# A decoder layer on one core: the experts' gate and up products turned round, and two tiles of the attention's output prepared before the attention ends

## The reference

```python
x = x + attn(_layernorm(x), W_qkv, W_out)           # 16 heads of 64, rotary, causal mask, softmax
x = x + xattn(_layernorm(x), ctx, ctx, Wq, ..., Wo) # a memory M per head, scanned over 64 context rows; out = M q, Wo, bo
x = x + ffn(_layernorm(x), router_w, router_b, we_gate, we_up, we_down)

# ffn: 8 experts, top 2 of them for each token
ff_gate = ragged_dot(sorted_tokens, we_gate, group_sizes)
ff_up = ragged_dot(sorted_tokens, we_up, group_sizes)
ff_out = ragged_dot(silu(ff_gate) * ff_up, we_down, group_sizes)
out = zeros.at[sorted_token_idx].add(ff_out * sorted_weights[:, None])
```

## Time and profile before

| | |
|---|---|
| median of 3 runs | 2870.94 us (2869.32 to 2877.44) |
| the profiled execution | 2874.91 us |
| its span | 2873.2 us |
| mean granted clock of TensorE | 0.973 |
| PE, DVE, ACT, POOL busy | 93%, 70%, 56%, 51% of the span |

### The profile page before, as it was taken

The page is one execution under the profiler, slowest core; times in us unless marked ns, Lnnn a source line. Parts: engine busy times, 40 slices in busy tenths (PEclk is TensorE's granted clock), DMA queues, the critical chain, the costliest instruction groups (busy, mean ns, idle before and its releaser), DMA issues. The chain is left out here.

```text
span 2873.2 us, 48962 instructions
## 1 busy us (share of the span) xinstructions
PE 2665.0 (93%) x15375; PEld 2267.7 (79%) x15375; DVE 2000.5 (70%) x4223; ACT 1620.8 (56%) x3157; POOL 1468.0 (51%) x1676
## 2 busy tenths in 40 slices
PE   7999989999899999899998599999959999999997
PEld 5888878888788888788887487877748888888886
DVE  6777766777667777677777688978846556666655
ACT  3666666666656666566666333333336666666665
POOL 3676646676647675556565333434323444343434
PEclk9999999999999999999999799999979999999999
DMA  6654544444544444444444654544334443444433
GB/s 175 106 122 106 123 103 98 118 113 104 132 96 99 115 107 114 103 109 100 94 91 114 170 135 134 158 134 147 96 126 96 102 87 74 102 99 100 100 52 51
DMA packets 192360, 316.56 MB, mean 110 GB/s; under 512 B 60496, under 2 KB 106224, under 8 KB 189104
## 3 DMA queue, kind: packets, MB, share of 16 engines
q1 hardware_dynamic: 148656, 216.86, 31.6%
q0 software_dynamic: 43520, 97.46, 13.9%
HBM read 241.08 MB, written 75.17 MB: 110 GB/s over the span
## 5 line engine op out<-in xcount | busy, mean ns | idle before, releaser
L1095 ACT ACTIVATE a_pt<-a_PT 128x512 fp32r<-128x512 f32 (+3 forms) x768 | 350.4, 491 | 449.9 <-PE a_PT L962 443.3
L1226 DVE TENSOR_TENSOR a_pt<-a_PT,a_pt 128x512 fp32r<-128x512 f32 (+3 forms) x768 | 401.5, 550 | 155.2 <-ACT a_pt L1095 150.7
L1216 DVE CUSTOM_DVE_ANT_0 a_S<-a_S,a_mask 128x1024 f32<-128x1024 f32 (+7 forms) x512 | 387.5, 757 | 72.5 <-PE a_S L951 71.1
L1084 ACT ACTIVATE a_pb<-a_S,a_nmax 128x1024 f32<-128x1024 f32 (+7 forms) x512 | 381.0, 744 | 36.5 <-DVE a_nmax L1216 36.5
L962 PE MATMUL a_PT<-early_ident,a_pb 128*128 128x128 f32 x2304 | 345.0, 276 | 51.2 <-DVE a_pt L1226 50.9
L962 PEld LDWEIGHTS a_PT<-early_ident,a_pb 128*128 128x128 f32 x2304 | 275.9, 142 | 112.4 <-issue 58.5
L979 PE MATMUL a_O<-a_pt,a_v 128*128 128x256 f32 (+1 forms) x2560 | 346.5, 283 | 17.8 <-DVE a_xt L1201 16.8
L979 PEld LDWEIGHTS a_O<-a_pt,a_v 128*128 128x128 f32 x2560 | 330.4, 193 | 31.2 <-DVE a_xt L1201 24.0
L2193 DVE TENSOR_TENSOR e_w<-early_stage,e_w 128x1024 fp32r<-128x1024 f32 x238 | 280.6, 1220 | 65.0 <-ACT e_w L2142 64.9
L950 PE MATMUL a_S<-a_kh,a_qs 128*128 128x512 f32 (+3 forms) x768 | 286.7, 373 | 10.6 <-DMA a_kl<-a_rot 8.8
L951 PE MATMUL a_S<-a_kl,a_qs 128*128 128x512 f32 (+3 forms) x768 | 259.0, 349 | 0.0
(11 more groups left out here) (305 smaller groups left out, 6890.2 us busy)
## 6 DMA issues: line engine op xcount, KB each, us to landing
a_qs<-a_rot SPq DMA_DIRECT2D x256, 128.0 KB, 2.4
a_kh<-a_rot SPq DMA_DIRECT2D x256, 128.0 KB, 2.4
a_kl<-a_rot SPq DMA_DIRECT2D x256, 128.0 KB, 2.4
e_rows<-scr_hs SPq DMA_DIRECT2D x40, 516.0 KB
scr_attT<-a_ot SPq DMA_DIRECT2D x256, 64.0 KB, 2.2
m_att<-scr_attT SPq DMA_DIRECT2D x32, 512.0 KB
m_rb<-scr_rinv SPq DMA_DIRECT2D x64, 256.0 KB
early_stage<-in_wqk POOLq DMA_DIRECT2D x31, 512.0 KB
```

Source lines behind the costliest of these rows:

```text
L1084: act.activation(pb[u % 2][:, 0:cols], S[u % 2][:, 0:cols], ACT.Exp, bias=nmax[:, u % GU:u % GU + 1], scale=-1.0, accum_out=rsum[:, b % 2, ...
L1095: act.activation(pt[u % 2][:, 0, 4 * s:4 * s + m, (qt % 2) * P:(qt % 2 + 1) * P], PT[(k + s) % 2][:, 0:m * P].rearrange("p (k q) -> p k q" ...
L1216: dve.tensor_tensor_reduce(out=sc, in0=sc, in1=mask[:, T - cols:T], scale=-1.0, scalar=-MASKED, op0=ALU.add, op1=ALU.min, accum_out=nmax[: ...
L1226: dve.tensor_tensor(pt[u % 2][:, 1, 4 * s:4 * s + m, q], PT[(k + s) % 2][:, 0:m * P].rearrange("p (k q) -> p k q", k=m), pt[u % 2][:, 0, 4 ...
```

## The change

In the attention and the memory stage:

- The tensor `rot` becomes `early["rot"]` and outlives the attention; the memory stage's `ap` (the split attention output of two tiles) lies in it.
- The last batch's sums are turned in unit U + 2 instead of U + 4.
- In units U - 13 and U - 11 SP loads the attention output and the sums of tiles 0 and 1 (`load_front`) into buffers that are free by then; POOL scales them in units U - 8 and U - 6, ACT makes the high parts in U + 1 and U + 2, DVE the low parts in U + 2 and U + 3.
- The four pieces of W_out are split in the last units too: high parts by ACT in U - 7, U - 5, U - 3, U - 1, low parts by POOL in U - 5, U - 3, U - 1, U + 1, into `xT`. POOL's loop runs to U + 2 for it.
- The memory stage no longer does any of this, PE waits for the constants only before the memory products, and in the second step PE transposes the first tile's n2 behind the first half of the second tile's product with W_out, not ahead of it. SP loads x of tiles 0 and 1 and then tile 2's attention output first.

In the experts:

- Gate and up have the weights as the stationary operand and 256 rows moving, so their results have features along the partitions and need no transposes for down. A half h is now 256 features of all 256 rows, not 128 rows.
- The engines' orders within a block change, and POOL's `fetch(0)` comes before `add_rows(0)`. DVE's wait for `added` with the small work comes before `mult(j, 0)`.

The diff, cut to its core:

```diff
         def sums_turn(u):
-            if u >= GU * G and u % (GU * G) == 4:
+            if u == U + 2:
+                return B - 1
+            if GU * G <= u < U and u % (GU * G) == 4:
                 return u // (GU * G) - 1
...
+        FRONT_IN = (U - 13, U - 11)
+        FRONT_SCALE = (U - 8, U - 6)
+        TAIL_HIGH = (U - 7, U - 5, U - 3, U - 1)
+        TAIL_LOW = (U - 5, U - 3, U - 1, U + 1)
...
+            def load_front(j):
...
+                sp.dma_start(front_rows(j), dram["attT"][j:j + 1, :, :].rearrange("o p (f t) -> p (o f) t", t=P)
+                             ).then_inc(s_first[j], 16)
+                for a in range(2):
+                    sp.dma_start(front_sums(j)[a * 64:(a + 1) * 64, :],
+                                 dram["rinv"][j, a:a + 1, :].rearrange("a n -> (a n)").partition_broadcast(64)
+                                 ).then_inc(s_first[j], 16)
             for u in range(U + 6):
                 if values_turn(u - 1) is not None:
                     store(values_turn(u - 1))
+                if u in FRONT_IN:
+                    load_front(FRONT_IN.index(u))
...
+            def front_scale(j):
+                gp.wait_ge(s_first[j], 48)
+                rows = front_rows(j)
+                gp.tensor_tensor(rows, rows, front_sums(j).rearrange("p (f t) -> p f t", t=P),
+                                 ALU.mult).then_inc(s_fscale, 1)
+            def tail_low(k):
+                gp.wait_ge(s_wmhi, k + 1)
+                gp.tensor_tensor(xT[:, 1, k, :], tail(k), xT[:, 0, k, :].bitcast(F32),
+                                 ALU.subtract).then_inc(s_wmlo, 1)
-            for u in range(U):
+            for u in range(U + 2):
...
+                if u in FRONT_SCALE:
+                    front_scale(FRONT_SCALE.index(u))
+                if u in TAIL_LOW:
+                    tail_low(TAIL_LOW.index(u))
...
             # attention, ACT
+                if u in TAIL_HIGH:
+                    tail_high(TAIL_HIGH.index(u))
+                if u in (U + 1, U + 2):
+                    front_high(u - U - 1)
             # attention, DVE
+                if u in (U + 2, U + 3):
+                    front_low(u - U - 2)
...
             # memory stage, PE
-            pe.wait_ge(s["pool"], 18)
+                second = isinstance(r, int) and r * QT + i == 1
+                if here(r, i - 1) and not second:
                     turn("n", 1, n2[:, (i - 1) % 2, :], "n2")
...
                     att_out(0, 4)
+                if second:
+                    turn("n", 1, n2[:, (i - 1) % 2, :], "n2")
...
             # experts, POOL
-                wait_alone(gp, s["y"], 2 * j + 1 + CR, s["any"])
-                add_rows(0)
                 wait_alone(gp, s["ix"], j + 2, s["any"])
                 wait_alone(gp, s["wlo0"], 2 * j + 4, s["any"])
                 fetch(0)
+                wait_alone(gp, s["y"], 2 * j + 1 + CR, s["any"])
+                add_rows(0)
...
             # experts, PE
+            def product(j, k, out, h, sem):
+                if h == 0:
+                    pe.wait_ge(s[f"wlo{k}"], 2 * j + 2)
+                if k == 0:
+                    pe.wait_ge(s["tlo"], 2 * j + RT + CR)
+                    pe.wait_ge(s["mul"], 2 * j + h - 1 + CR)
+                for f in range(2 * h, 2 * h + 2):
+                    for e in range(ET):
+                        c = e * D + f * P
+                        mm = parts(out[h][:, f % 2 * BLK:(f % 2 + 1) * BLK], lambda a: w[:, k, a, c:c + P],
+                                   lambda a: hT[:, a, e, :], e)
                 mm.then_inc(s[sem], 1)
+            def down(j, t, h):
+                pe.wait_ge(s["alo"], 2 * j + h + 1 + CR)
...
                 product(j, 0, pG, 0, "G")
+                product(j, 0, pG, 1, "G")
                 product(j, 1, pU, 0, "U")
-                product(j, 0, pG, 1, "G")
-                turn_act(j, 0)
                 product(j, 1, pU, 1, "U")
+                down(j, 0, 0)
                 turn_rows(j + 1, 0)
-                down(j, 0, 0, 2)
-                turn_act(j, 1)
-                down(j, 0, 2, ET).then_inc(s["Y"], 1)
+                down(j, 1, 0)
                 turn_rows(j + 1, 1)
-                down(j, 1, 0, ET).then_inc(s["Y"], 1)
+                down(j, 0, 1)
+                down(j, 1, 1)
             # experts, ACT
                 silu(j, 0)
                 silu(j, 1)
+                weight_high(j + 1, 0, "G")
                 act_high(j, 0)
-                weight_high(j + 1, 0, "G")
+                act_high(j, 1)
                 turn_high(j + 1, 0)
                 act.wait_ge(s["arg"], j + 1)
                 act.activation(gate[:, :], arg[:, :], ACT.Tanh).then_inc(s["gate"], 1)
-                act_high(j, 1)
+                turn_high(j + 1, 1)
                 weight_high(j + 1, 1, "U")
                 act.wait_ge(s["wt"], j + 1)
                 row_out(j, 0)
-                turn_high(j + 1, 1)
                 row_out(j, 1)
                 weight_high(j + 1, 2, "Y")
             # experts, DVE
                 for h in range(2):
                     weight_low(j, 2, h)
-                mult(j, 0)
-                act_low(j, 0)
-                mult(j, 1)
                 dve.wait_ge(s["added"], j + 1)
...
                 keep_side(j + 1)
+                mult(j, 0)
+                act_low(j, 0)
                 weight_low(j + 1, 0, 0)
+                mult(j, 1)
+                act_low(j, 1)
                 turn_low(j + 1, 0)
-                act_low(j, 1)
+                weight_low(j + 1, 0, 1)
                 dve.wait_ge(s["gate"], j + 1)
                 dve.tensor_scalar(wt[:, :], gate[:, :], 0.5, 0.5, ALU.mult, ALU.add).then_inc(s["wt"], 1)
-                weight_low(j + 1, 0, 1)
+                turn_low(j + 1, 1)
                 for h in range(2):
                     weight_low(j + 1, 1, h)
-                turn_low(j + 1, 1)
```

More of the change, by code:

```diff
@@ L506, in attention_phase @@
         s_wm = rm.sem("wm")
+        s_wmhi = rm.sem("wmhi")
+        s_wmlo = rm.sem("wmlo")
+        s_first = [rm.sem(f"first{i}") for i in range(2)]
+        s_fscale = rm.sem("fscale")
+        s_fhi = rm.sem("fhi")
+        s_flo = rm.sem("flo")
         s_scan = rm.sem("scan")
@@ L731, in _ @@
                                  ).then_inc(s_k2, 16)
+            def load_front(j):
+                i = NG * GH // 2 - 1
+                if j == 0:
+                    for k in range(2):
+                        sp.wait_ge(s_xst[k], 16 * QT * (B - 1))
+                    for k in range(4):
+                        sp.wait_ge(s_ost[k], 16 * NPAIR // B // 4)
+                    sp.wait_ge(s_rst, 16)
+                    sp.wait_ge(s_zfull, zi[("q", i, 3)] + 1)
+                else:
+                    sp.wait_ge(s_radd, 4 * (i + 1))
+                sp.dma_start(front_rows(j), dram["attT"][j:j + 1, :, :].rearrange("o p (f t) -> p (o f) t", t=P)
[4 more added lines that the diff above has]
+                                 ).then_inc(s_first[j], 16)
             for u in range(U + 6):
@@ L1105, in key_root, with tail_high, front_high @@
                 act.activation(kst[1], kst[0], ACT.Sqrt).then_inc(s_ksd, 1)
+            def tail_high(k):
+                act.wait_ge(s_wm, 96)
+                act.activation(xT[:, 0, k, :], tail(k), ACT.Copy).then_inc(s_wmhi, 1)
+            def front_high(j):
+                act.wait_ge(s_fscale, j + 1)
+                for sl in range(2):
+                    act.wait_ge(s_stack[sl], 192 * (NG * GH // 2))
+                act.activation(front[:, j, 0, :, :], front_rows(j), ACT.Copy).then_inc(s_fhi, 1)
             key_root(0)
@@ L1697, in _ @@
             act.sem_inc(s["hT"], CR)
[L1698 to L1701, removed]
+            act.sem_inc(s["ahi"], CR + 2)
             def att_high(r, j):
                 t = r * QT + j
-                act.wait_ge(s["an"], t + 1)
+                act.wait_ge(s["an"], t - 1)
                 act.wait_ge(s["x2"], t - 1 + CR)
@@ L1736, in step @@
                 memory_high(1)
-                if here(r, i + 1):
+                if here(r, i + 1) and after(r, i + 1, 2):
                     att_high(r, i + 1)
@@ L1769, in _ @@
         def _(dve):
-            for k in ("x2", "x3", "alo", "nlo", "qn", "rt", "pos", "mwl"):
+            for k in ("x2", "x3", "nlo", "qn", "rt", "pos", "mwl"):
                 dve.sem_inc(s[k], CR)
+            dve.sem_inc(s["alo"], CR + 2)
             dve.sem_inc(s["st30"], 16)
@@ L1790, in centre @@
                 dve.wait_ge(s["wc"], n + 3)
[L1792 to L1795, removed]
             def att_low(r, j):
@@ L2073, in turn_rows @@
                 pe.wait_ge(s["rows"], 16 * (j + 1))
-                pe.wait_ge(s["tlo"], 2 * j + t + CR)
+                pe.wait_ge(s["tlo"], 2 * j + t - 1 + CR)
                 for e in range(ET):
-                    mm = pe.transpose(pT[1][:, e * P:(e + 1) * P], rows[:, t, e * P:(e + 1) * P], ident[:, :])
```

(10 more changed lines are left out.)

108 lines of the change are left out of this document (57 added, 51 removed).

## The result

The kernel after took 2916.36 us (median of 4 runs, 2910.89 to 2920.65), the kernel before beside it 2871.64: ratio 1.0151, 95% interval 1.0139 to 1.0163. It is 45 us slower where 15 less were forecast, and outside the range. The profiled execution took 2920.65, its span is 2918.9, against 2873.2 before.

What follows compares the result with a forecast made beforehand. PE was taken to bound the experts, with the new block at 18.4 us set by the chain through `added`. Experts -5, weight changes +3, boundary -13 made -15 against 2874.9: 2860, median 2857; whole range 2834 to 2892.

Steps and rivals of the forecast that it cites:

- PE's sum: Experts: two transpose groups go (-0.86), narrower gate and up products add 0.32; PE's block 17.98 instead of 18.52 us.
- The loop through `added`: Experts: down product, row output, stores, landing, DVE's wait, next down product take 18.4 us a block; -0.12 x 39 = -5.
- The price of a change of weights: Experts: at seven changes of expert the second store lands late, about 0.4 us each remaining; +3 in all.
- the second store taken as free: Experts: POOL's second store, tried at 10.48, was summed without blocking by DVE, in a block of 18.4 us.
- rival A: Experts: DVE's lowering blocks the second store, adding 0.8; block 19.2, +27 over 39 blocks, median 2888; chance 0.28.
- the landing: Experts: second store lands 4.9 us after its start, at 15.38; `added` follows by 0.2.
- The last leg: Experts: from `dest` to the next down product: 0.62, three operations together 2.04, and 0.2 for hand-overs.
- the boundary: Attention's end to memory stage: opening 4.7 us later, 18 won after it; net -13, bounds -9 and -18.
- The bounds, +1 and +7: Memory stage's opening, +4.7 us forecast: +1 if the main chain ends last, +7 at 2.83 per POOL operation.
- +22 to +25: Memory stage: PE turns the second tile's normalised rows this many us after the opening, instead of 41.9; -18.
- C: Experts: the chain doesn't bind and PE sets the block, 17.98; -21 there, -34 in all, median 2837; chance 0.25.
- D: Boundary gives nothing: POOL's tail at +7, loads late, PE cold; with block 18.4, median 2870; chance 0.07 including what else.

Runs made afterwards that it cites:

- e4: Kernel after with DVE waiting for both gate products before the second half of the down weights' lowering: 2893.7 us, ratio 1.0079 to the kernel before.
- e2: Kernel after with the expert stage of the kernel before, so the new boundary alone: 2874.4 us, ratio 1.0010 to the kernel before.
- e9: Kernel after, order kept, with the memory's store issued by SP instead of POOL: 2911.1 us, ratio 1.0128 to the kernel before.
- e5: Kernel after with POOL's last two scan rows and memory store ahead of the first tile's scaling: 2899.7 us, ratio 1.0096 to the kernel before.
- e8: e6 with POOL's scaling of the third tile ahead of its wait for the six constants: 2826.7 us, ratio 0.9845 to the kernel before.
- e3: Kernel after with DVE's wait for `added` and its small operations moved behind mult(j,1): 2846.6 us, ratio 0.9912 to the kernel before.
- e6: Kernel after with the changes of e3 and e5 together: 2834.0 us, ratio 0.9870 to the kernel before.

## Why the prediction was wrong

**What held.** PE's sum: 17.83 a block once nothing waits, 17.98 forecast. The 48 gate products in 5.68 (2453.31 to the first up product at 2458.99) are 0.118 apart; 96 of them are 11.36, so the narrow form costs 0.16 more and not 0.32, which is the whole difference. By the rule of the Trainium skill (TensorE: Matmul & The Clock Gate, Back-to-back issue gap) the estimate was 0.12 more and a block of 17.78: nearer in the difference, but the rule's spacing itself, 0.109, is further from the measured 0.118 than my 0.120 of the earlier trace rows. The loop through `added` was the right one, the order on ACT came as computed (weight_high at +4.46, row_out(0) at +6.26; 4.36 and 6.16 forecast), the first store was blocked (2.45), and the second was tried at 10.56 (10.48). The price of a change of weights was less than forecast: from first down product to first down product the blocks exceed their median by 2.3 in all, and by 1.1 before the change, so 1.2 more where the sum has 3.

**The step that failed first: the second store taken as free.** "Mine is 0.09 after" was written of rival A and is what happened: the store was tried 0.04 to 0.24 after DVE's second lowering had begun, in 37 of the 38 blocks seen whole (it took 2.43 to 2.64 there; 1.58 in the one other). The deciding margin was under the errors of the sum, and every error in it was systematic, so the 39 blocks fell on one side together; the forecast should have been A. The Trainium skill (SBUF — State Buffer, SBUF: two separate sides) says that whichever starts first, an operation of DVE with two inputs in SBUF or one of GpSimd that reads SBUF, holds the port that they share for its whole length, and the other waits. For DVE's side the trace agrees: the store takes 2.62 beside the lowering and 1.58 without (e4). For the store the other side isn't seen: where it began 0.18 ahead, DVE's pair of lowerings kept its 2.36 and the store took 1.73. A's price, 0.8, was 0.60.

**The second: the landing.** I added 4.9, the median over all transfers of `out`, and 0.2. Unblocked, from the store's start to `dest` is 5.31, where 5.1 was forecast, and blocked 5.91. In the trace of before the profile tells the landing of second stores alone, 4.27 after the first store's start; in e4 the second store begins 2.76 after the first and, unblocked, lands at 5.24 (median). Whether the nearer first store delays it, no run shows. The last leg, from `dest` to the down product, took 3.01; the prediction's terms for it add up to 2.86, and their sum of 18.44 was rounded to 18.4. The sum: 18.44 + 0.08 (start) + 0.60 (blocked) + 0.21 (landing and hand-over) + 0.15 (last leg) = 19.48, against 19.51 measured. The three small terms all went the same way; with the rounding they are 0.48, and in a loop that is walked 39 times that is 19 us.

**Third: the boundary, -13 forecast, about +3 measured** (e2). The opening was forecast at 1599.9 and came at 1613.49:
- The memory's store went at 1603.69, not 1596.4 (the terms as written, 1570 + 25.8, give 1595.8: the 0.6 of the store's second half is in the 1599.9 twice). The broadcast load that was said to "queue behind that stack" at no cost let POOL start at 1573.20 and not 1567. It landed 14.2 (median) after its issue, behind 3 MB of memory weights that POOL had asked for 8 us earlier, with the DMA engines full up to then (share 1.01 from 1553 to 1573). And one scan step's row of additions took 5.07 instead of 2.29. These are 6.2 and 2.8; the rest of POOL's chain was 1.1 shorter than summed, so that 7.3 remain against 1596.4.
- Those 2.8 stand beside DVE's low parts of tiles 0 and 1, which the change itself put there. The last addition, 128x16, took 3.00 instead of 0.22 and ended 0.08 behind the second of them; in e9 another small operation took 2.91 instead of 0.22 and again ended 0.08 behind that pair. It looks like the clash that stretched the experts' stores, a second time; no run takes it away alone.
- From POOL's store to the opening I took what SP's store had taken, 2.9, and 0.6 for its second half; it is 9.8. That is 6.3.

The bounds, +1 and +7, had only the operations' durations in them and none of these. Why it matters is order: POOL was free for its last scan rows at 1552 and held them behind a load that came at 1573 (e5).

After the opening, -18 was forecast and -14.4 came. The place is the one the text passed over in a sentence: POOL's first multiplication waits for the constants, and DVE holds the second tile's sum behind what hangs on it. e8 takes it away: 22.4, inside "+22 to +25".

**The rivals.** A had the mechanism, the sign, and 0.28; its median, 2888, was 28 short, because it stood on a boundary of -13 (16 of the 28) and on the small terms of the loop (12). C, with 17.98, is what e3 shows for another order of DVE's work. D's "the boundary gives nothing" was true beside A, a pair to which no number was given; the two would have made 2901. The forecast's own terms add up to 2856 in medians, not 2857; it changes nothing.

## What to carry to other kernels

When a wait is moved ahead of work that feeds the bounding engine, walk the whole loop from that engine back to itself, and price it with rows of exactly those instructions; if it comes within a few tenths of the bound, expect it to bind: the small terms that were left out or rounded were 0.48 a block in sum, and all on the long side. The same wait behind the second multiplication turned 45 us of loss into 25 of gain. And an in-order engine that gets a job waiting on a DMA should first do what it already has the data for, above all a store on which a stage's end waits.

## What was not expected

- An indirect store blocked by DVE takes 1.04 longer to issue (2.62 against 1.58), but its data are in only 0.60 later.
- A stage that ends with POOL's own store opened 9.8 us after it was issued, four times within 0.02; with the same store from SP 6.6; with the last store a 64 KB one from SP 2.9 to 3.0.
- The features' product form is worth more than its sum said: PE's block fell by 0.70 (18.53 to 17.83), against 0.54 by the sum, and 256-column products with new weights each ran at 0.118, without a loss of clock (1.00 in the stretch).
- In the kernel after, DVE's scaling of the second tile's rows took 2.30 (1638.59 to 1640.89), where the first tile's took 0.55, while a multiplication of POOL that had started 0.3 earlier ran to 1640.61. This is 1.75 of the way to the turn; the same 2.3 stand in e2 to e6, e8 and e9, and 2.35 before the change; no experiment took them away.
